# Layer norm rows, z and its scaled copy: from VectorE to GpSimd, in a fused two-layer decoder kernel

## The reference

```python
def _layernorm(x, axis=-1, eps=1e-05):
    m = jnp.mean(x, axis=axis, keepdims=True)
    v = jnp.var(x, axis=axis, keepdims=True)
    return (x - m) / jnp.sqrt(v + eps)

x = x + _L0_attn_ref(_layernorm(x), ...)      # 16 heads
x = x + _L0_xattn_ref(_layernorm(x), ctx, ...)  # 1 head
x = x + _L0_ffn_ref(_layernorm(x), ...)
x = x + _L1_attn_ref(_layernorm(x), ...)      # 1 head, causal
x = x + _L1_xattn_ref(_layernorm(x), ctx, ...)  # 16 heads
x = x + _L1_ffn_ref(_layernorm(x), ...)
```

## Time and profile before

| | us |
|---|---|
| median of 3 runs | 435.55 (434.41 to 436.92) |
| the profiled execution, its own time | 432.98 |
| its span, from first to last instruction | 431.2 |
| PE busy | 357.8 (83%) |
| DVE busy | 323.7 (75%) |
| ACT busy | 262.1 (61%) |
| POOL busy | 141.9 (33%) |

### The profile page before, as it was taken

The page is one execution under the profiler, slowest core; times in us unless marked ns, Lnnn a source line. Parts: engine busy times, 40 slices in busy tenths (PEclk is TensorE's granted clock), DMA queues, the critical chain, the costliest instruction groups (busy, mean ns, idle before and its releaser), DMA issues.

```text
span 431.2 us, 9413 instructions
## 1 busy us (share of the span) xinstructions
PE 357.8 (83%) x3164; PEld 208.3 (48%) x3164; DVE 323.7 (75%) x929; ACT 262.1 (61%) x582; POOL 141.9 (33%) x223
## 2 busy tenths in 40 slices
PE   2454899999999969599987589999989888769793
PEld 1342544454544348469976423444444443326583
DVE  5331888999899346725795687989999994489996
ACT  2130688888888835566554306887878788655531
POOL 3550555446400001301233432456654222221111
PEclk9985999999999997999998956999999999969987
DMA  6213124222360000000000231221221100000003
GB/s 193 74 51 98 45 73 110 76 64 57 106 179 3 2 0 2 2 2 0 2 0 2 74 100 48 51 64 46 70 64 45 45 2 3 0 0 2 0 2 97
DMA packets 36260, 19.98 MB, mean 46 GB/s; under 512 B 4038, under 2 KB 35318, under 8 KB 36214
## 3 DMA queue, kind: packets, MB, share of 16 engines
q1 hardware_dynamic: 35894, 19.25, 16.7%
q10 hardware_dynamic: 320, 0.13, 0.1%
HBM read 5.58 MB, written 1.05 MB: 15 GB/s over the span
## 4 chain that ended last, share of the span: by engine, by line
PE 43%; DVE 33%; ACT 7%; issue 6%; POOL 5%; SPq 3%; DMA 2%; DVEq 0%; ACTq 0%; POOLq 0%
DVE negmax_sb L785 13%; PE pv_ps L1188 10%; PE s_ps L1142 9%; DVE late_sb L1015 5%; PE prep_ps L1098 3%; SPq L405 3%; ACT probT_sb L521 3%; PE s_ps L1238 3%; PE prep_ps L1102 2%; PE s_ps L1151 2%; PE out_ps L1270 2%; POOL rstd_sb L445 2%; PE s_ps L1287 2%; DVE xn_sb L762 2%; PE s_ps L1253 1%
## 5 line engine op out<-in xcount | busy, mean ns | idle before, releaser
L785 DVE TENSOR_REDUCE negmax_sb<-s_ps 128x2 bf16<-128x512 f32 x256 | 162.4, 688 | 35.9 <-PE s_ps L1151 35.8
L521 ACT ACTIVATE probT_sb<-s_ps 128x512 f32<-128x512 f32 x256 | 142.2, 597 | 29.9 <-PE s_ps L1142 27.8
L1151 PE MATMUL s_ps<-stack_sb 62*128 62x256 bf16 x512 | 93.6, 288 | 3.5 <-DMA stack_sb<-parts_sb 3.1
L1142 PE MATMUL s_ps<-stack_sb 63*128 63x256 bf16 x512 | 90.3, 276 | 7.1 <-ACT probT_sb L521 3.2
L1188 PE MATMUL pv_ps<-probT_sb,v_aug_sb 128*32 128x256 f32 x1024 | 69.4, 389 | 0.8 <-ACT probT_sb L521 0.8
L1142 PEld LDWEIGHTS s_ps<-stack_sb 63*128 63x128 bf16 x512 | 30.3, 94 | 65.6 <-ACT probT_sb L521 40.3
L443 POOL TENSOR_SCALAR rstd_sb<-mv_sb 128x2 f32<-128x2 f32 x32 | 7.1, 222 | 124.6 <-DVE mv_sb L754 124.5
L543 ACT ACTIVATE qkf_sb<-prep_ps,b_qkv_sb 128x256 f32<-128x256 f32 x56 | 23.9, 470 | 26.7 <-PE prep_ps L1102 19.7
L1188 PEld LDWEIGHTS pv_ps<-probT_sb,v_aug_sb 128*32 128x32 f32 x1024 | 26.9, 110 | 25.8 <-issue 13.7
L1151 PEld LDWEIGHTS s_ps<-stack_sb 62*128 62x128 bf16 x512 | 30.6, 96 | 11.6 <-DVE negmax_sb L785 6.4
L845 DVE SCALAR_TENSOR_TENSOR x_all_sb<-out_ps,den_inv_sb,x_all_sb 128x128 f32<-128x128 f32 x32 | 9.8, 346 | 25.1 <-PE out_ps L1270 24.9
(11 more groups left out here) (177 smaller groups left out, 659.6 us busy)
## 6 DMA issues: line engine op xcount, KB each, us to landing
stack_sb<-parts_sb SPq DMA_DIRECT2D x192, 64.0 KB, 2.1
x_all_sb<-x SPq DMA_DIRECT2D x4, 256.0 KB, 3.5
ctxT_sb<-ctxT SPq DMA_DIRECT2D x2, 512.0 KB, 5.0
f_w_sb<-f_w SPq DMA_DIRECT2D x2, 512.0 KB, 4.0
out<-x_all_sb SPq DMA_DIRECT2D x4, 256.0 KB, 2.4
d_w_sb<-d_w SPq DMA_DIRECT2D x2, 320.0 KB, 3.6
w_att_sb<-w_att SPq DMA_DIRECT2D x2, 256.0 KB, 3.8
b_vo_sb<-b_vo SPq DMA_DIRECT2D x1, 512.0 KB, 4.9
```

Source lines behind the costliest of these rows:

```text
L521: act.activation(probT[:, c % 8], s2_ps[c % 2][:, :, :], ACT.Exp, scale=DH ** -0.5).then_inc(exp_ready, 1)
L785: dve.tensor_reduce(negmax[:, n % 2, :, max_column(max_head(h))], s1_ps[c % 3][:, :, :], axis=AX.X, op=ALU.max, negate=True).then_inc(max_ ...
L1142: i = pe.matmul(s2_ps[c % 2][:, k, :], stack[rows, s3, 1, h // 2, k * P:(k + 1) * P], stack[rows, s3, 0, h // 2, :], start=True, stop=True)
L1151: i = pe.matmul(s1_ps[c % 3][:, k, :], stack[rows, s3, 0, hp, k * P:(k + 1) * P], stack[rows, s3, 1, hp, :], start=True, stop=True)
```

## The change

`ln_apply`, `z_apply` and the `xr` part of `z_route` (now `z_scale`) become helpers that take the engine. GpSimd calls `ln_apply` right behind its reciprocal root for n = 2 to 10 and n = 27 to 31, 14 items; VectorE keeps n = 0 and 1 and all items of the one-head loop. GpSimd calls `z_apply` behind its reciprocal root and `z_scale` behind the root of the norm for b = 0 to 5; b = 6 and 7 stay on VectorE. Each call is two instructions, so 52 instructions move. No other engine's list changes.

```diff
+        Z_POOLED = B - 2
+        def ln_apply(eng, n):
+            u = n % 2
+            eng.wait_ge(rstd_ready, n + 1)
+            if n >= 2:
+                eng.wait_ge(xnT_psum, n - 1)
+            for k in range(NT):
+                i = eng.tensor_scalar(xn[:, u, k, :], x_all[:, tiles(n).start + k, :], mv[:, u, k, 0:1], rstd[:, u, k:k + 1],
+                                      ALU.subtract, ALU.mult)
+                if k == NT - 1:
+                    i.then_inc(xn_ready, 1)
+        def pooled(n):
+            return 2 <= n <= B + AHEAD or n >= 3 * B + AHEAD_C
+        def z_apply(eng, b):
+            eng.wait_ge(rn_step, 5 * b + 2)
+            for k in range(NT):
+                i = eng.tensor_scalar(z[:, b % 2, k, :], x_all[:, last_tiles(b).start + k, :], z_mv[:, b, k, 0:1], z_rstd[:, b, k:k + 1],
+                                      ALU.subtract, ALU.mult)
+            i.then_inc(z_ready, 1)
+        def z_scale(eng, b):
+            eng.wait_ge(rn_ready, b + 1)
+            if b >= 2:
+                eng.wait_ge(xrT_psum, b - 1)
+            for k in range(NT):
+                i = eng.tensor_scalar(xr[:, b % 2, k, :], z[:, b % 2, k, :], rnorm[:, b, k:k + 1], None, ALU.mult)
+            i.then_inc(xr_ready, 1)
...
                 pool.tensor_tensor(rstd[:, u, :], rstd[:, u, :], minus_half[:, 0:NT], ALU.pow).then_inc(rstd_ready, 1)
+                if pooled(n):
+                    ln_apply(pool, n)
...
                 pool.tensor_tensor(rs, rs, minus_half[:, 0:NT], ALU.pow).then_inc(rn_step, 1)
+                if b < Z_POOLED:
+                    if b >= 2:
+                        pool.wait_ge(s_tok_ready, NT * (b - 1))
+                    z_apply(pool, b)
...
                 pool.tensor_tensor(rn, rn, minus_half[:, 0:NT], ALU.pow).then_inc(rn_ready, 1)
+                if b < Z_POOLED:
+                    z_scale(pool, b)
...
-                dve.wait_ge(rn_ready, b + 1)
-                if b >= 2:
-                    dve.wait_ge(xrT_psum, b - 1)
-                for k in range(NT):
-                    i = dve.tensor_scalar(xr[:, b % 2, k, :], z[:, b % 2, k, :], rnorm[:, b, k:k + 1], None, ALU.mult)
-                i.then_inc(xr_ready, 1)
+                if b >= Z_POOLED:
+                    z_scale(dve, b)
...
-                        if h == 2 and ln is not None:
-                            ln_apply(ln)
+                        if h == 2 and ln is not None and not pooled(ln):
+                            ln_apply(dve, ln)
...
-                            if h == 7:
-                                z_apply(i - 2 - B)
+                            if h == 7 and i - 2 - B >= Z_POOLED:
+                                z_apply(dve, i - 2 - B)
```

More of the change, by code:

```diff
@@ L880, in z_norm_stats @@
                     dve.bn_aggr(z_mv[:, b, k, :], z_stats[:, b % 2, k, :]).then_inc(z_mv_ready, 1)
[L882 to L887, removed]
             def z_route(b):
@@ L938, in _ @@
                         for n in ahead(i, 3):
-                            ln_apply(n)
+                            ln_apply(dve, n)
                         if i == B:
```

## The result

The changed kernel takes 444.39 us in the median (444.22 to 448.26, 4 runs), the kernel before 436.24 beside it (434.41 to 436.97, 4 runs). The ratio is 1.0215, with a 95% interval of 1.0149 to 1.0280: slower by about 8 us (8.15 between the medians, 9.4 by the ratio), where 435.3 had been forecast and the range ended at 440.3. The profiled execution is the longest of the four (448.26, span 446.4), 3.9 us above the median, so its stretches are read for where the time went, and the sums go by medians and ratios.

A forecast was written before the change was run, and what follows sets the result against it. VectorE was full only from about 287 to 356 us, within a ring of waits through PE and POOL. Terms +0.28, -0.11, -0.40, -0.20, +0.62, -0.40 summed to -0.2 us: 432.8 profiled, 435.3 for the median; range 430.0 to 440.3.

The forecast's parts named there:

- The price on POOL: A GpSimd TENSOR_SCALAR of 128x128 at 0.45 us for xn and z, 0.86 a pair; xr 0.38, 0.72 a pair.
- The ring: Second 16-head loop: closed chain of waits from PE's xn transposes through VectorE, POOL's root and xn, 14.89 us a step.
- The ring's first leg: Second 16-head loop: from the xn transposes to the row maximum of h = 13, 7.57 us of PE's own work.
- T: Start of PE's transposes of xn in a step of the second 16-head loop, 305.23 us in the profile before.
- First loop 0, and two gains of 0.2: First 16-head loop: PE's step stays 13.26 us; steps 0 and 6 gain 0.2 us each from an earlier xn.
- xn pair +0.26, entries +0.26, +0.10, +0.26: Second loop: xn on POOL takes 0.86 us for 0.60, +0.26 a step; steps 8, 9, 10 add +0.26, +0.10, +0.26.
- z pair worth 0: Second loop, steps 10 to 14: z's 0.50 us off VectorE only lengthens its 0.43 us wait for PE, gaining 0.
- xr -0.11, through the split's end: Second loop: products end 0.15 us behind POOL's split, so xr off VectorE brings the next row maximum only 0.11 us forward.
- Rival C: Second loop: the first product also falls behind POOL's split, +0.35 us in three steps, 436.4; chance 0.49 together with the forecast.
- Ring step 15.03: Second loop: a step from xn transposes to xn transposes grows from 14.89 to about 15.03 us, +0.28 for two turns.
- Steps 13 and 14, -0.40 and -0.20: Second loop: xr off VectorE gains 0.40 us in step 13, without a POOL split, and 0.20 in step 14.
- Rival B: Both loops: xn on POOL is late, 1.20 us a pair, +1.0 a step in the second; +3.8, 439.3; chance 0.21.

The follow-up runs named there:

- alone-run: Changed kernel with only xn of the first loop (n = 2 to 10) left on POOL, z, xr and later xn on VectorE: 439.29 us, ratio 1.0116.
- run with idle transposes: Changed kernel plus six unread identity transposes on TensorE before each wait for a pooled xn of n = 27 to 31: 441.03 us, ratio 1.0134.

## Why the prediction was wrong

**The price on POOL** is the step that failed: "251 + 126 x 0.83 is 0.36 us ... so 0.45 each and 0.86 for a pair". It measured 0.80 each and 1.58 a pair, above the upper bound of 1.4, and 0.60 and 1.19 for xr, for 0.38 and 0.72. The bound was no bound: two-input instructions on 256 elements (724 ns) and casts say nothing of what an element costs in a TENSOR_SCALAR. The one row of that operation, 251 ns on 2 elements, named the fixed part only, and that alone should have made the slope the widest unknown.

**The ring's first leg**, "7.57 us of PE to the row maximum", was a second error. In the kernel before the chain goes through VectorE alone there, as shown above, and not through the transposes T. PE's leg decides only once z has left VectorE or xn comes late. So "VectorE, all the time", which the prediction turned down, was right but for POOL's root.

**First loop 0, and two gains of 0.2.** The cover was read rightly: "a pair over 1.14 us would be late here in five steps". At 1.58 it is late by 0.44, and a step is 0.52 longer. The alone-run loses 5 us here and behind it.

**xn pair +0.26, entries +0.26, +0.10, +0.26.** Right place, wrong size: xn is 0.98 longer. In the run with idle transposes steps 8 and 9 are 0.84 and 0.97 longer than before (15.38 and 14.42 for 14.54 and 13.45, by the starts of their transposes).

**z pair worth 0.** Wrong, by a misread row: "issue" in the chain taken for idle time. It brings the products 0.24 us forward, seen in the version with z and xr.

**xr -0.11, through the split's end.** Wrong in its mechanism. A product ends with the split instruction that it meets, not with the split. POOL's split ended at T + 11.4 with the clock held up (323.30), 1.8 us later than before, and the products ended at T + 9.18, 0.6 earlier. Of this, 0.44 is that they started earlier (T + 7.73 for 8.17), and 0.15 that the first slipped in free and the second met L373, the split's second instruction (1.45 us for the pair, 1.60 before). Rival C had the pattern, and priced only one of its directions.

**Ring step 15.03.** With the clock held up it is 15.17, and that this is close is luck: two errors cancel. Up to the end of the products it is 0.59 us shorter (9.18 for 9.77), where 0.16 longer was forecast (9.78 + 0.15 = 9.93). Behind it, it is 0.88 longer (5.99 for 5.11), where 0.02 shorter was forecast: +0.25 for xn and -0.27 for the xr pair. In the changed kernel it is 15.88 and 17.07.

**Not in the prediction at all:** the granted clock. Longer waits for xn were priced at their own length. The fall behind them costs another 1.3 us in a step, and 0.8 through the lock.

**Steps 13 and 14, -0.40 and -0.20.** By the starts of xr's transposes they take 12.66 and 12.72 us before, and 12.27 and 12.22 with the idle transposes: -0.39, as forecast, and -0.50, more than it.

**Rival B** was the right one, at a price of 1.20. It named the place (xn late), the point of about 1.0 us from which it decides, and 439.3; it had no term for the clock and too small a one for the first loop. The +7.5 that the prediction gave for a pair at its upper bound, with a chance of 0.08, comes nearest to the measured 8 to 9.

One thing stays open. Two executions of one program can differ by 1.5 us in step 0 alone, where the granted clock from 52 to 56 us is 1.00 in one and 0.57 in the other (both of the version with z and xr, spans 430.0 and 431.5). The transposes of step 0 had waited 0.71 us for xn in both, so the length of that wait does not decide it. The profiled execution of the kernel before had its full clock there, that of the changed one did not (0.50 from 56 to 58 us). What decides it no run here shows.

## What to carry to other kernels

Before work is moved to GpSimd, price it by a row of the same operation at the same size, or measure it; a row of the same operation at another size gives the fixed cost only. Take slack on an engine from the timeline, not from an "issue" piece of the chain. Before an instruction is freed or moved, look whether the chain of waits holds it at all. Where a wait for a moved result grows on TensorE, add what the clock may cost behind it; and where VectorE and GpSimd both work from SBUF, ask which instruction meets which, since some hundredths of a us decide whether 0.3 or 1.2 us are paid.

## What the hardware showed

- A GpSimd TENSOR_SCALAR on 128x128 f32 costs 0.81 us with two operations and two columns, 0.64 with two constants, 0.60 with one operation and one column, against 0.29 for a plain copy of the same size; VectorE's pair of the first kind takes 0.60.
- VectorE's TENSOR_SCALAR with one input from SBUF was held too: 1.43 us for a pair of 0.47, beside a POOL instruction of 1.16. A product of 0.28 took 1.12 to 1.23 when it met such an instruction early, and ended about 0.15 us behind it.
- TensorE's granted clock was at half behind waits for xn of 1.54 and 1.91 us, and at full behind such waits of 1.22, 1.48 and 1.49. Six idle transposes in the wait kept it at full in steps 11 and 12. In step 8 it was at half ahead of the wait, in the kernel before too, and at step 0 it fell in one execution and not in another behind the same wait of 0.71.
